# A decoder block on one core: value product and softmax sums of all attentions in one matmul group, causal maxima over 384 adjacent columns

## The chip, the cores and the metric

The kernel runs on one core of one Trainium2 chip. The metric is the device time of one execution in microseconds. Engines are called TensorE (PE in the rows; PEld is its weight load), VectorE (DVE), ScalarE (ACT), GpSimd (POOL) and SyncE (SP); SPq and ACTq in the rows are DMA issues.

## What is computed

Two decoder layers over 16 sequences of 256 tokens of 256 features, each stage followed by a residual addition and a layer norm without weights. Three of the stages are attentions:

```python
# L0 self: differential attention, 32 query heads, 8 key and 8 value heads, head size 16, causal
aw = softmax(where(tril, q @ k.T / 4, -inf))
aw = aw.reshape(B, 16, 2, S, S); aw = aw[:, :, 0] - lam * aw[:, :, 1]
y = ((aw @ v * (1 - LAMBDA_INIT)) @ Wproj) @ Wproj
# L0 cross: 16 heads of 16 against a context, no mask
out = (softmax(Q @ K.T / 4) @ V) @ w_o.T + b_o
# L1 cross: the same with biases, causal
```

The other stages (a mixture of experts behind the first cross attention, a state space layer, a feed forward with low rank experts at the end) are not touched.

## The kernel before

The stages stand one behind the other, in this order of their names: self, cross, moee, ssm, causal, ffn. `cross_attention` builds both cross and causal. In each attention a batch is one sequence. Every engine has its own program: the function `batches` calls `body(st)` once a batch, a batch in the middle in a loop of two batches an iteration, and `body` runs over the pairs i of the batch, 16 in self and 8 in cross and causal, and places the steps at fixed i. So the order on an engine is written by hand, and engines meet at semaphores alone. The stages of the work are shifted against each other: `st.has(1)` steps work on the next batch (maxima), `st.has(3)` steps on the one three ahead (projections), `st.has(-1)` and `st.has(-2)` steps on earlier ones (output product, layer norm). In self the pairs of one batch's scores begin in the middle of the body (`now`, LAG = 8).

For each pair TensorE makes the scores twice. `max_scores` writes them with queries on the partitions into one of two buffers `max_ps`; in the causal attentions the two query halves have 128 and 256 keys, and the second half begins at column 256, so a gap of 128 columns is between them. A bf16 product adds the mask on the diagonals. VectorE reduces them to `neg_max` (`take_max`; two reductions in the causal ones, of 128 and 256 columns for each of two heads). After four pairs `transpose_max` turns the maxima, ScalarE keeps them (`keep_max`), and a small DMA on ScalarE's queue (`load_row`) adds them as a row to `q_stack`. `scores` then makes the transposed scores with that row, in the single buffer `score_ps`; ScalarE writes the exponential into `probs` (`exponential`), and GpSimd clears what lies above the diagonal in the causal ones (`mask_probs`).

`weighted` multiplies a group of two pairs with matmuls of 32 output rows, one for each quarter of the partitions. A group writes its values with `v_pad` (parts 0 and 1) into the left half of `out_ps`, and the sums of its probabilities with `ones` (parts 2 and 3) into the right half. `v_pad` has for each of the two parities of a head 16 columns of values and 16 of zeros, so that two groups, one after the other, add up to 32 rows. Two groups are one tile. `keep_weighted` on ScalarE copies `out_ps` to `comb`, which frees `out_ps` for the next tile; `normalize` on VectorE takes the reciprocal of the sums and multiplies; `part_o` on GpSimd splits the result in a high and a low part for the output product (`output`, `output_1`).

On SP's queue `body` writes in cross and causal the finished rows of an earlier batch, then saves the split k, loads stacks, saves the split q and, after both saves have landed, loads the next half of the stacks (L361, L364).

## Time and profile before

| | us |
|---|---|
| median of 3 runs | 2770.53 |
| lowest and highest run | 2765.45, 2774.43 |
| span of the profiled execution | 2765.9 |
| window in the steady part of self, 100 to 660 | 560 |
| window in the steady part of cross, 820 to 1050 | 230 |
| window in the steady part of causal, 2240 to 2450 | 210 |
| TensorE busy, whole span | 2451.4 |
| VectorE busy | 1928.7 |
| ScalarE busy | 1439.0 |
| GpSimd busy | 1560.7 |

The self stage takes the time up to about 724 us, cross 724 to about 1110, causal from about 2165 to 2515. Busy times of TensorE overlap between matmuls; what a matmul group takes is best read as the distance of two starts.

### The profile page before, as it was taken

The numbers are of one execution on the slowest core, as the hardware profiler recorded it, in microseconds if no ns is written. First come the engines' busy times: TensorE is split into PE (matmuls) and PEld (weight loads), VectorE is DVE, ScalarE is ACT, GpSimd is POOL, SyncE is SP. The second block draws the span as 40 slices with busy tenths as digits, with TensorE's granted clock in tenths as the row PEclk, the third lists the DMA queues.
The fourth block names the chain that finished last, engine by engine and source line by source line (L and its number), as shares of the span: only waits on it lengthen the run. The fifth ranks groups of instructions, "written<-read, shape, count | busy, mean of one in ns | idle before, by whom it ended". The sixth has DMA issues, their size and how long they took to land. (4 is left out here: it accounts for less than half of the span.)

```text
span 2765.9 us, 66315 instructions
## 1 busy us (share of the span) xinstructions
PE 2451.4 (89%) x24760; PEld 2025.2 (73%) x24760; DVE 1928.7 (70%) x3095; ACT 1439.0 (52%) x2255; POOL 1560.7 (56%) x1873
## 2 busy tenths in 40 slices
PE   5999999999589998898999994888896799997998
PEld 4676666676466665898999993677775577765998
DVE  2567666677367786364888885999985377775776
ACT  2565565565356665433665663656563355553333
POOL 3666565666345543056666664777765477764443
PEclk9999999999799999899999997999997899998999
DMA  8565555562477873024666663111000877761111
GB/s 200 124 152 138 130 146 117 144 146 68 122 193 203 208 193 93 31 89 160 217 230 221 216 217 118 37 39 47 24 13 29 238 192 207 209 146 35 58 57 50
DMA packets 228039, 363.48 MB, mean 131 GB/s; under 512 B 52848, under 2 KB 157168, under 8 KB 220272
## 3 DMA queue, kind: packets, MB, share of 16 engines
q1 hardware_dynamic: 207248, 281.28, 38.9%
q0 software_dynamic: 17376, 78.13, 8.0%
q8 instruction: 153, 2.51, 0.4%
q10 hardware_dynamic: 3200, 1.05, 0.2%
q14 instruction: 62, 0.51, 0.1%
HBM read 231.68 MB, written 133.69 MB: 132 GB/s over the span
## 5 line engine op out<-in xcount | busy, mean ns | idle before, releaser
L1278 ACT ACTIVATE self_probs<-self_score_ps 128x768 f32<-128x768 f32 x256 | 207.7, 811 | 218.7 <-PE self_score_ps L1180 215.7
L1494 POOL TENSOR_SCALAR_AFFINE_SELECT self_probs<-self_probs 128x512 f32<-128x512 f32 x256 | 167.7, 656 | 217.6 <-ACT self_probs L1278 217.4
L1415 DVE TENSOR_REDUCE self_neg_max<-self_max_ps 128x2 f32<-128x256 f32 x256 | 108.2, 422 | 227.1 <-PE self_max_ps L1166 223.6
L722 DVE TENSOR_REDUCE cross_neg_max<-cross_max_ps 128x4 f32<-128x1024 f32 x128 | 155.9, 1222 | 70.6 <-PE cross_max_ps L500 69.6
L632 ACT ACTIVATE cross_probs<-cross_score_ps 128x1024 f32<-128x1024 f32 x128 | 131.1, 1024 | 92.9 <-PE cross_score_ps L522 92.8
L1416 DVE TENSOR_REDUCE self_neg_max<-self_max_ps 128x2 f32<-128x512 f32 x256 | 174.5, 682 | 0.0
L2206 POOL TENSOR_TENSOR moee_h_lo<-moee_h,moee_h_hi 128x512 fp32r<-128x512 f32 x78 | 112.0, 1436 | 93.0 <-ACT moee_h_hi L1943 92.3
L3501 POOL TENSOR_TENSOR ffn_g_lo<-ffn_g_full,ffn_g_hi 128x512 fp32r<-128x512 f32 x64 | 82.2, 1284 | 129.4 <-ACT ffn_g_hi L3387 117.0
L1943 ACT ACTIVATE moee_h_hi<-moee_h 128x512 fp32r<-128x512 f32 x110 | 69.5, 632 | 164.2 <-DVE moee_h L2109 158.7
L632 ACT ACTIVATE causal_probs<-causal_score_ps 128x768 f32<-128x768 f32 x128 | 103.9, 811 | 95.0 <-PE causal_score_ps L522 94.9
L1180 PE MATMUL self_score_ps<-self_q_stack,self_k_stack 49*128 49x128 f32 (+1 forms) x1024 | 131.3, 336 | 24.7 <-issue 10.3
L79 PE MATMUL moee_g_ps<-moee_x_hi,moee_in_hi 128*128 128x256 f32 x440 | 132.2, 300 | 11.1 <-DVE moee_x_lo L2096 6.9
L1180 PEld LDWEIGHTS self_score_ps<-self_q_stack,self_k_stack 49*128 49x128 f32 x1024 | 79.0, 191 | 73.6 <-issue 40.0
L2109 DVE TENSOR_TENSOR moee_h<-moee_u_ps,moee_silu 128x512 f32<-128x512 f32 x110 | 75.6, 687 | 81.2 <-PE moee_u_ps L81 77.0
L1160 PE MATMUL self_max_ps<-self_k_stack,self_q_stack 48*128 48x128 f32 (+1 forms) x1024 | 108.2, 291 | 23.0 <-POOL self_k_stack L1525 22.0
L815 POOL TENSOR_SCALAR_AFFINE_SELECT causal_probs<-causal_probs 128x512 f32<-128x512 f32 x128 | 85.0, 664 | 75.7 <-ACT causal_probs L632 71.8
L79 PE MATMUL moee_y_ps<-moee_out_hi,moee_h_hi 128*128 128x256 f32 x440 | 125.3, 285 | 1.5 <-DVE moee_out_lo L2061 1.5
L81 PE MATMUL moee_g_ps<-moee_x_hi,moee_in_lo 128*128 128x256 f32 x440 | 126.4, 287 | 0.0
L80 PE MATMUL moee_g_ps<-moee_x_lo,moee_in_hi 128*128 128x256 f32 x440 | 126.3, 287 | 0.0
L2149 POOL DMA_INDIRECT x_tiles<-kept_x,moek_slot x64 | 65.8, 1029 | 106.7 <-issue 103.0
L79 PE MATMUL moee_u_ps<-moee_x_hi,moee_in_hi 128*128 128x256 f32 x440 | 125.5, 285 | 0.0
L81 PE MATMUL moee_u_ps<-moee_x_hi,moee_in_lo 128*128 128x256 f32 x440 | 125.0, 284 | 0.0
(500 smaller groups left out, 9667.4 us busy)
## 6 DMA issues: line engine op xcount, KB each, us to landing
self_q<-self_q_split SPq DMA_DIRECT2D x48, 512.0 KB, 3.2
self_q_raw<-self_q SPq DMA_DIRECT2D x32, 768.0 KB, 7.9
cross_stacks<-cross_qk SPq DMA_DIRECT2D x64, 384.0 KB, 6.6
causal_stacks<-causal_qk SPq DMA_DIRECT2D x64, 384.0 KB, 6.6
moe_y_tiles<-lasting_y_out SPq DMA_DIRECT2D x55, 256.0 KB, 2.5
mid<-lasting_y_out SPq DMA_DIRECT2D x48, 256.0 KB, 2.2
x_tiles<-zeros SPq DMA_DIRECT2D x16, 624.0 KB, 4.5
moee_xT<-x_tiles SPq DMA_DIRECT2D x39, 256.0 KB, 7.1
```

What stands on the lines that cost most here:

```text
L79: pe.matmul(out, a[0], b[0], start=start, stop=False, **kw)
L80: pe.matmul(out, a[0], b[1], start=False, stop=False, **kw)
L81: return pe.matmul(out, a[1], b[0], start=False, stop=stop, **kw)
L632: nc.scalar.activation(probs[i // 2][:, a, :, lo:], score_ps[:, :, lo:], ACT.Exp, scale=HD ** -0.5).then_inc(prob_ready, 1)
L722: last = dve.tensor_reduce(neg_max[p][:, tile, :, col % 4, :], bank[:].rearrange("p a (q k) -> p a q k", q=QT), AX.X, ALU.max, negate=True)
L1160: last = pe.matmul(max_ps[i % 2][:, ab, q * S:q * S + (q + 1) * P], q_stack[rows, 4 * tile + c, q * P:(q + 1) * P], k_stack[p][rows, tile, ...
L1180: last = pe.matmul(score_ps[:, ab, j * S + k * P:(j + 1) * S], k_stack[p][rows, tile, k * P:(k + 1) * P], q_stack[rows, 4 * tile + c, k * P:],
L1278: nc.scalar.activation(probs[g % 4][:, a, :, P:], score_ps[:, :, P:], ACT.Exp, scale=HD ** -0.5).then_inc(prob_ready, 1)
L1415: dve.tensor_reduce(neg_max[:, tile, :, c, 0:1], bank[:, :, 0:P], AX.X, ALU.max, negate=True)
L1416: dve.tensor_reduce(neg_max[:, tile, :, c, 1:2], bank[:, :, S:2 * S], AX.X, ALU.max, negate=True).then_inc(max_kept, 1)
L1494: pool.affine_select(diagonal, diagonal, [[0, 2], [0, 2], [1, P]], ALU.is_ge, zero, base=0, channel_multiplier=-1).then_inc(prob_masked, 1)
L2206: pool.tensor_tensor(h_lo[p][f][:].rearrange("p j s -> p (j s)"), h[f][:], h_hi[p][f][:].bitcast(F32).rearrange("p j s -> p (j s)"), ALU.s ...
```

## The change

The 16 columns of `v_pad` that were zero get ones in every second column, beginning with the number of the tile. A group's product with `v_pad` now gives 16 rows of values and 16 rows that hold the sum in every second row. The groups of the two parities no longer add up; the first writes the left half of `out_ps`, the second the right half. The four matmul parts of `weighted` become two. To bring the halves together, ScalarE copies `out_ps` with its halves exchanged and scaled by a 0/1 column (`cross_weighted`, now placed ahead of `exponential` at its pair), and VectorE adds to it the other rows out of `out_ps` (`merge`, a scalar_tensor_tensor); this frees `out_ps`. GpSimd adds the sums of two tiles (`add_sums`), VectorE takes one reciprocal for both (`invert`) and `normalize` spreads a tile's half over the rows with a stream_shuffle and multiplies. `part_o` of two tiles stands at adjacent pairs.

In the causal attentions the 256 keys of the second query half now begin at column 128, and one reduction takes three blocks of 128 columns for two heads into `block_max`; after four pairs `join_max` takes the smaller negated maximum of the two blocks of the second half, and `transpose_max` waits for it.

The core of the diff (the self stage has the same edits of its functions; of it only the bodies of VectorE and GpSimd are shown, last):

```diff
@@ -531,23 +539,16 @@
                 if g == 0:
                     pe.wait_ge(v_padded, 2 * st.done(d))
                 if par == 0 and (tile or st.has(d - 1)):
-                    pe.wait_ge(comb_ready, st.at(d) * 2 + tile)
-                for part in range(4):
-                    k = part % 2
-
+                    pe.wait_ge(merged_ready, st.at(d) * 2 + tile)
+                for k in range(QT):
                     first_q = P if causal and k == 1 else 0
                     cols = slice((1 - k) * S + first_q, (2 - k) * S)
                     for quad in range(4):
                         rows = slice(32 * quad, 32 * quad + 32)
-                        if part < 2:
-                            lhs = v_pad[p][:, k, tile * 4 + quad, par, :, :].rearrange("p a e -> p (a e)")
-                            out0 = 0
-                        else:
-                            lhs, out0 = ones[:, par, :], S
-                        last = pe.matmul(out_ps[rows, out0 + first_q:out0 + S], lhs,
+                        lhs = v_pad[p][:, k, tile * 4 + quad, par, :, :].rearrange("p a e -> p (a e)")
+                        last = pe.matmul(out_ps[rows, par * S + first_q:(par + 1) * S], lhs,
                                          probs[g][:, quad % 2, quad // 2, cols],
-                                         start=(par == 0 and part == 0),
-                                         stop=(par == 1 and part == 3), skip_group_check=True)
+                                         start=k == 0, stop=k == QT - 1, skip_group_check=True)
                 last.then_inc(pv_done, 1)
@@ -632,12 +633,12 @@
                 nc.scalar.activation(probs[i // 2][:, a, :, lo:], score_ps[:, :, lo:],
                                      ACT.Exp, scale=HD ** -0.5).then_inc(prob_ready, 1)
 
-            def keep_weighted(st, d, tile):
+            def cross_weighted(st, d, tile):
                 act.wait_ge(pv_done, st.at(d) * 4 + 2 * tile + 2)
                 if st.has(d - 1):
                     act.wait_ge(o_ready, st.at(d) * 2 + tile - 1)
-                nc.scalar.activation(comb[tile][:].rearrange("p a s -> p (a s)"), out_ps[:],
-                                     ACT.Identity).then_inc(comb_ready, 1)
+                nc.scalar.activation(crossed[tile][:, ::-1, :], out_ps[:].rearrange("p (a s) -> p a s", s=S),
+                                     ACT.Identity, scale=halves[:, 1:2]).then_inc(crossed_ready, 1)
 
             def finish_rows(st):
                 n, p = st.done(-2), st.parity(-2)
@@ -651,6 +652,10 @@
 
             def body(st):
                 for i in range(PAIRS):
+                    if i == 2 and st.has(-1):
+                        cross_weighted(st, -1, 1)
+                    if i == 6 and st.has(0):
+                        cross_weighted(st, 0, 0)
                     if st.has(0):
                         exponential(st, i)
                     if i == 0 and st.has(0):
@@ -707,32 +708,61 @@
             for t in range(2):
                 dve.memset(v_pad[t][:], 0.0).then_inc(v_zeroed, 1)
             dve.wait_ge(v_zeroed, 2)
+            for t in range(2):
+                for tile in range(2):
+                    for par in range(2):
+                        ones = v_pad[t][:, :, 4 * tile:4 * tile + 4, par, 1 - par, tile::2]
+                        last = dve.memset(ones, 1.0)
+                last.then_inc(v_zeroed, 1)
 
             def take_max(st, i):
                 n, p, (tile, par, a, col) = st.at(1) * PAIRS + i, st.parity(1), place(i)
                 dve.wait_ge(max_done, n + 1)
-                if i % 4 == 0 and st.has(-1):
-                    dve.wait_ge(maxT_done, st.at(-1) * 2 + tile + 1)
                 bank = max_ps[i % 2]
                 if causal:
-                    dve.tensor_reduce(neg_max[p][:, tile, :, col % 4, 0:1], bank[:, :, 0:P], AX.X, ALU.max, negate=True)
-                    last = dve.tensor_reduce(neg_max[p][:, tile, :, col % 4, 1:2], bank[:, :, S:2 * S], AX.X, ALU.max,
-                                             negate=True)
+                    if i % 4 == 0 and (i or st.has(0)):
+                        dve.wait_ge(max_joined, st.at(1) * 2 + tile)
+                    last = dve.tensor_reduce(block_max[:, :, col % 4, :],
+                                             bank[:, :, 0:3 * P].rearrange("p a (j t) -> p a j t", t=P),
+                                             AX.X, ALU.max, negate=True)
                 else:
+                    if i % 4 == 0 and st.has(-1):
+                        dve.wait_ge(maxT_done, st.at(-1) * 2 + tile + 1)
                     last = dve.tensor_reduce(neg_max[p][:, tile, :, col % 4, :],
                                              bank[:].rearrange("p a (q k) -> p a q k", q=QT),
                                              AX.X, ALU.max, negate=True)
                 last.then_inc(max_kept, 1)
 
+            def join_max(st, tile):
+                dve.wait_ge(max_kept, st.at(1) * PAIRS + 4 * tile + 4)
+                if st.has(-1):
+                    dve.wait_ge(maxT_done, st.at(-1) * 2 + tile + 1)
+                dve.tensor_tensor(neg_max[st.parity(1)][:, tile], block_max[:, :, :, 0:2], block_max[:, :, :, 0::2],
+                                  ALU.min).then_inc(max_joined, 1)
+
+            def merge(st, d, tile):
+
+                dve.wait_ge(crossed_ready, st.at(d) * 2 + tile + 1)
+                if st.has(d - 1):
+                    dve.wait_ge(sums_ready, st.at(d))
+                    dve.wait_ge(o_ready, st.at(d) * 2 + tile - 1)
+                dve.scalar_tensor_tensor(merged[tile][:], out_ps[:].rearrange("p (a s) -> p a s", s=S),
+                                         halves[:, 0:1], crossed[tile][:], ALU.mult, ALU.add).then_inc(merged_ready, 1)
+
+            def invert(st, d):
+                dve.wait_ge(sums_ready, st.done(d))
+                dve.reciprocal(inv_sum, sums).then_inc(inv_ready, 1)
+
             def normalize(st, d, tile):
 
                 n = st.at(d) * 2 + tile
-                dve.wait_ge(comb_ready, n + 1)
-                dve.reciprocal(inv_sum[:, tile, :], comb[tile][:, 1, :]).then_inc(inv_ready, 1)
-                dve.wait_ge(inv_ready, n + 1)
+                dve.wait_ge(inv_ready, st.done(d))
+                dve.memset(gate[:], 0.0)
+                dve.stream_shuffle(crossed[tile][:, 1, :], inv_sum, [HD + tile] * HD + [tile] * HD).then_inc(scale_ready, 1)
+                dve.wait_ge(scale_ready, n + 1)
                 if st.has(d - 1):
                     dve.wait_ge(olo_ready, n - 1)
-                dve.tensor_tensor(o_full[:, tile, :], comb[tile][:, 0, :], inv_sum[:, tile, :],
+                dve.tensor_tensor(o_full[:, tile, :], merged[tile][:, 0, :], crossed[tile][:, 1, :],
                                   ALU.mult).then_inc(o_ready, 1)
 
             def norm_rows(st):
@@ -763,8 +793,18 @@
                 for i in range(PAIRS):
                     if st.has(1):
                         take_max(st, i)
+                    if causal and i % 4 == 3 and st.has(1):
+                        join_max(st, i // 4)
+                    if i == 2 and st.has(-1):
+                        merge(st, -1, 1)
+                    if i == 6 and st.has(0):
+                        merge(st, 0, 0)
                     if i == 3 and st.has(-2):
                         norm_rows(st)
+                    if i == 4 and st.has(-1):
+                        invert(st, -1)
+                    if i in (5, 6) and st.has(-1):
+                        normalize(st, -1, i - 5)
                     if i == 5 and st.has(3):
                         dve.wait_ge(xhi_ready, st.done(3))
                         dve.tensor_tensor(x_lo[:].rearrange("p k s -> p (k s)"), misc[:],
@@ -772,10 +812,6 @@
                                           ALU.subtract).then_inc(xlo_ready, 1)
                     if i == 5 and st.has(-2):
                         shift_rows(st)
-                    if i == 4 and st.has(-1):
-                        normalize(st, -1, 1)
-                    if i == 7 and st.has(0):
-                        normalize(st, 0, 0)
 
             run(dve, body)
 
                                 ).then_inc(zeroed, 1)
...
+            def add_sums(st, d):
+                pool.wait_ge(merged_ready, st.done(d) * 2)
+                if st.has(d - 1):
+                    pool.wait_ge(inv_ready, st.done(d - 1))
+                pool.tensor_tensor(sums, merged[0][:, 1, :], merged[1][:, 1, :], ALU.add).then_inc(sums_ready, 1)
...
+                    if i == 2 and st.has(-1):
+                        add_sums(st, -1)
                     if i == 0 and st.has(3) and st.has(2):
                         split_context(st)
                     if i == 2 and st.has(1):
                         pad_v(st)
-                    if i == 3 and st.has(-1):
-                        part_o(st, -1, 0)
-                    if i == 5 and st.has(-1):
-                        part_o(st, -1, 1)
+                    if i in (6, 7) and st.has(-1):
+                        part_o(st, -1, i - 6)
                     if i == 4 and st.has(-2):
                         pool.wait_ge(eps_ready, st.done(-2))
@@ -1455,21 +1522,30 @@
                 for i in range(PAIRS):
                     if st.has(1):
                         take_max(st, i)
+                    if i % 4 == 3 and st.has(1):
+                        join_max(st, i // 4)
                     if i == 1 and st.has(3) and st.has(2):
                         lower_x(st)
                     if i == 3 and st.has(-1):
                         norm_rows(st)
                     if i == 5 and st.has(-1):
                         shift_rows(st)
-                    if i in (3, 7, 11) and st.has(0):
-                        normalize(st, 0, i // 4 + 1)
+                    if i in (2, 6, 10) and st.has(0):
+                        merge(st, 0, i // 4 + 1)
+                    if i in (4, 11) and st.has(0):
+                        invert(st, 0, i // 8)
+                    if i in (5, 6) and st.has(0):
+                        normalize(st, 0, i - 5)
+                    if i == 11 and st.has(0):
+                        normalize(st, 0, 2)
+                        normalize(st, 0, 3)
+                    if i == 14 and st.has(1):
+                        merge(st, 1, 0)
...
-                    if i == 15 and st.has(1):
-                        normalize(st, 1, 0)
@@ -1546,8 +1628,10 @@
                     d, pair = now(st, i)
                     if st.has(d):
                         mask_probs(st, d, pair)
-                    if i in (0, 4, 8, 12) and st.has(0):
-                        part_o(st, 0, i // 4)
+                    if i in (2, 10) and st.has(0):
+                        add_sums(st, 0, i // 8)
+                    if i in (6, 7, 12, 13) and st.has(0):
+                        part_o(st, 0, (6, 7, 12, 13).index(i))
                     if i in (6, 8) and st.has(3):
                         split_q(st, i // 2 - 3)
```

VectorE in self, a batch's normalization at pair 11 between the maxima of pairs 11 and 12, before (`self_neg_max<-self_max_ps` are the maxima, the line is that of the kernel before):

```order
L1415 TENSOR_REDUCE self_neg_max<-self_max_ps 128x2
L1416 TENSOR_REDUCE self_neg_max<-self_max_ps 128x2
L1423 RECIPROCAL self_inv_sum<-self_comb 128x256
L1427 TENSOR_TENSOR self_o_full<-self_comb,self_inv_sum 128x256
L1415 TENSOR_REDUCE self_neg_max<-self_max_ps 128x2
```

and after, from the merge of pair 10 to the maxima behind pair 11 (lines of the kernel after):

```order
L1478 SCALAR_TENSOR_TENSOR self_merged<-self_out_ps,lasting_halves,self_crossed 128x512
L1460 TENSOR_REDUCE self_block_max<-self_max_ps 128x2x3
L1468 TENSOR_TENSOR self_neg_max<-self_block_max 128x16
L1483 RECIPROCAL self_merged<-self_merged 128x256
L1489 MEMSET self_gate 128x1
L1490 STREAM_SHUFFLE self_crossed<-self_merged 128x256
L1494 TENSOR_TENSOR self_o_full<-self_merged,self_crossed 128x256
L1489 MEMSET self_gate 128x1
L1490 STREAM_SHUFFLE self_crossed<-self_merged 128x256
L1494 TENSOR_TENSOR self_o_full<-self_merged,self_crossed 128x256
L1460 TENSOR_REDUCE self_block_max<-self_max_ps 128x2x3 x3
```

One reciprocal and one multiply of a tile stood there; now a join, a reciprocal for two tiles, and shuffle and multiply for each of them stand between two maxima, and a merge stands ahead of the maxima of pair 11.

ScalarE in cross, from the transposed maxima of pair 0 to pair 3, before:

```order
L672 ACTIVATE cross_v_full<-cross_misc 128x512
L632 ACTIVATE cross_probs<-cross_score_ps 128x1024
L622 DMA cross_stacks<-cross_max_row 1x8x128 x2
L632 ACTIVATE cross_probs<-cross_score_ps 128x1024
L639 ACTIVATE cross_comb<-cross_out_ps 128x512
L632 ACTIVATE cross_probs<-cross_score_ps 128x1024 x2
```

and after:

```order
L677 ACTIVATE cross_v_full<-cross_misc 128x512
L633 ACTIVATE cross_probs<-cross_score_ps 128x1024
L623 DMA cross_stacks<-cross_max_row 1x8x128 x2
L640 ACTIVATE cross_crossed<-cross_out_ps,lasting_halves 128x2x256
L633 ACTIVATE cross_probs<-cross_score_ps 128x1024 x3
L613 ACTIVATE cross_max_row<-cross_max_ps 16x128
```

The copy of `out_ps` (L639, now L640) has moved ahead of the exponential of pair 2.

## Rows read from the trace of the kernel before

**Rows 1.** The page, part 1: busy us, share of the span, instructions.
```profile
PE 2451.4 (89%) x24760; PEld 2025.2 (73%) x24760; DVE 1928.7 (70%) x3095; ACT 1439.0 (52%) x2255; POOL 1560.7 (56%) x1873
```

**Rows 2.** Windows: length, then PE, PEld, DVE, ACT, POOL busy, PEclk, DMA share, GB/s.
```profile
100.00:660.00 560.00, 530.23 (x6861) 388.12 (x6859) 381.03 (x681) 333.13 (x502) 348.74 (x452) 0.96 0.57 135
...
820.00:1050.00 230.00, 221.00 (x2726) 159.39 (x2722) 182.75 (x232) 148.42 (x221) 114.23 (x164) 1.00 0.77 198
...
2240.00:2450.00 210.00, 206.91 (x2682) 156.24 (x2682) 153.20 (x295) 125.28 (x227) 158.95 (x235) 1.00 0.78 204
```

**Rows 3.** Timeline, self PE: start us, us, engine, line, out<-in, xcount [idle before <-releaser].
```profile
405.27 0.86 PE L1205 MATMUL self_out_ps<-self_probs,self_v_pad 128*32 128x256 f32 x16
405.94 0.83 PE L1205 MATMUL self_out_ps<-self_probs,lasting_ones 128*32 128x256 f32 x16
406.71 0.50 PE L1180 MATMUL self_score_ps<-self_q_stack,self_k_stack 49*128 49x128 f32 x4
...
408.19 0.50 PE L1180 MATMUL self_score_ps<-self_q_stack,self_k_stack 49*128 49x128 f32 x4 [0.32 <-ACT self_probs L1278]
```

**Rows 4.** Timeline, cross PE, one weighted group.
```profile
909.34 1.07 PE L547 MATMUL cross_out_ps<-cross_probs,cross_v_pad 128*32 128x256 f32 x16
910.23 1.05 PE L547 MATMUL cross_out_ps<-cross_probs,lasting_ones 128*32 128x256 f32 x16
```

**Rows 5.** Groups of DVE in self, 200:600: busy us, mean ns | idle before.
```profile
L1416 DVE TENSOR_REDUCE self_neg_max<-self_max_ps 128x2 f32<-128x512 f32 x154 | 105.0, 682 | 0.0
L1423 DVE RECIPROCAL self_inv_sum<-self_comb 128x256 f32<-128x256 f32 x38 | 66.3, 1745 | 0.0
L1415 DVE TENSOR_REDUCE self_neg_max<-self_max_ps 128x2 f32<-128x256 f32 x154 | 65.0, 422 | 126.2 <-PE self_max_ps L1166 123.1 <-PE self_max_ps L1142 2.5
...
L1437 DVE TENSOR_TENSOR self_r<-self_misc,self_x_res 128x512 f32<-128x512 f32 x10 | 6.8, 681 | 0.0
```

**Rows 6.** Timeline, self ACT around pair 5.
```profile
391.91 2.06 ACT L1269 ACTIVATE self_q_stack<-self_q_raw 128x1024 fp32r<-128x1024 f32 x1
393.86 0.63 ACT L1301 ACTIVATE self_q_split<-self_q_full 128x512 fp32r<-128x512 f32 x1
394.38 0.81 ACT L1278 ACTIVATE self_probs<-self_score_ps 128x768 f32<-128x768 f32 x1
```

**Rows 7.** Timeline, self: POOL and PE at the edge of a batch.
```profile
416.62 1.96 POOL L1525 CAST self_k_stack<-self_k_raw 128x1024 fp32r<-128x1024 f32 x1
...
418.72 0.50 PE L1160 MATMUL self_max_ps<-self_k_stack,self_q_stack 48*128 48x128 f32 x4 [1.33 <-POOL self_k_stack L1525]
```

**Rows 8.** Timeline, cross: SP and ACT queues, then PE at the next pair 4.
```profile
914.36 0.51 SPq L396 DMA_DIRECT2D kept_x<-lasting_y_out  x1
...
918.33 0.43 SPq L375 DMA_DIRECT2D cross_qk<-cross_q_split  x1
...
925.95 0.81 SPq L364 DMA_DIRECT2D cross_stacks<-cross_qk  x2
...
919.56 1.38 ACTq L622 DMA_DIRECT2D cross_stacks<-cross_max_row  x1
...
926.31 0.50 PE L522 MATMUL cross_score_ps<-cross_stacks 49*128 49x256 f32 x4 [0.55 <-DMA cross_stacks<-cross_max_row]
```

**Rows 9.** Windows of 2 and 3 us, columns as in rows 2.
```profile
418.00:420.00 2.00, 1.28 (x11) 0.98 (x11) 1.75 (x4) 0.58 (x2) 1.53 (x3) 0.99 0.00 0
420.00:422.00 2.00, 2.00 (x15) 1.27 (x18) 0.78 (x3) 1.41 (x2) 0.94 (x3) 0.50 0.00 0
...
903.00:906.00 3.00, 2.11 (x38) 1.16 (x32) 2.89 (x8) 0.70 (x1) 0.58 (x1) 1.00 0.99 353
```

**Rows 10.** Timeline, self PE in its last batches and at its end.
```profile
645.61 0.51 PE L1180 MATMUL self_score_ps<-self_q_stack,self_k_stack 49*128 49x128 f32 x4 [0.35 <-ACT self_probs L1278]
...
649.44 0.50 PE L1180 MATMUL self_score_ps<-self_q_stack,self_k_stack 49*128 49x128 f32 x4 [0.24 <-ACT self_probs L1278]
...
715.46 0.55 PE L79 MATMUL self_misc<-self_wo_hi,self_o_hi 128*128 128x256 f32 x1 [4.45 <-POOL self_o_lo L1505]
```

137 lines of the change are left out of this document (84 added, 53 removed).

## The prediction

> **What bounds the kernel now.** I read the page's busy shares first, then the stage windows, then the timeline of one batch on each engine, and last the queues. TensorE is busy 89% of the span [rows 1], and in the steady windows of self and cross attention 530 of 560 us and 221 of 230 us; the causal one is the same with 207 of 210 us [rows 2]. A reader sees an engine with next to no idle time, so work taken from it should show. But the windows also say how far the others are: VectorE is busy 183 of 230 us in cross, and the DMA engines 0.77 of it [rows 2]. So the question is how soon something else is late.
>
> **What TensorE loses.** In self attention the product with v_pad starts at 405.27, that with the ones at 405.94, the next scores at 406.71 [rows 3]. The second product goes, so a weighted group saves 0.67 us, the distance of the two starts. In cross attention all blocks are 256 columns wide and it is 910.23 - 909.34 = 0.89 us [rows 4]. There are 128 groups in self (16 batches, 8 each), 64 in cross, 64 in causal, whose shapes are those of self: 128 x 0.67 + 64 x 0.89 + 64 x 0.67 = 186 us leave the engine. The causal maxima keep the same matmuls and only move their columns together: nothing.
>
> **What the other engines get.** Maxima: the two reductions of a pair, 0.422 + 0.682 us [rows 5], become one of 768 columns. 256 more columns cost 0.26, so 0.94; as the two now overlap by some 0.17 (the starts follow each other faster than the durations say), it saves about 0.08 a pair. Every four pairs a join of 16 columns is added behind a wait on VectorE's own last reduction: by the reduction of 256 columns [rows 5] under 0.42; being tiny, I take 0.2. Merge: 512 columns out of PSUM, as L1437, 0.68 [rows 5], on VectorE, once a tile. Reciprocals halve: 1.745 once for two tiles [rows 5]. Shuffle: no row has one. It moves 256 columns, so between 0.2 and 0.7 (a reduction of 256 and an operation of 512 columns [rows 5]), taken 0.42, with as much for the multiply behind its wait. GpSimd gets an add of 256 columns for two tiles (below the 1.96 of its 1024-column cast [rows 7]; a fourth of it and a start, 0.7) and loses as much in the v copy. ScalarE does the same copy as before, but ahead of the exponential and not behind it. Summed, VectorE has about as much as before (4 merges, 4 joins and 4 shuffles against 2 reciprocals and 16 x 0.08), but in lumps.
>
> **Self attention, walked through one batch.** A pair with a group takes 2.42 us now and 1.75 after; scores cannot follow closer than 408.19 - 406.71 = 1.48, because they wait for the exponential [rows 3]. *Pairs 3 to 8* lose three groups, 2.0 us. At pair 5 ScalarE has a sort of 2.06 and a rounding of 0.63 before the exponential of pair 6 [rows 6]; that exponential is nearly late today, and now the copy of 0.6 (as the rounding of 512 columns [rows 6]) stands ahead of it, so group 5 gives back all it saves and 0.35 more. VectorE has from pair 3 to 6 a norm, an inversion, two normalizations and a merge between its maxima; the transposed maximum of pair 8 waits 0.35 for the join. I keep 0.65 of the 2.0. *Pairs 9 to 15* lose four groups, 2.7 us. At pair 11 VectorE now runs join, inversion and two normalizations without a maximum between them: 0.2 + 1.75 + 2 x 0.84 = 3.6 us against 2.2. The maxima of pair 12 queue behind it and hold both PSUM buffers, so TensorE waits 1.5 before the maxima of pair 14; the output product then waits 0.5 for the second o_lo. I keep 0.5. *The edge and pairs 0 to 2* lose one group, 0.67; the maxima there already wait 1.33 for GpSimd's sort of k, which follows the last exponential and not TensorE [rows 7], so 0.5 of it only lengthens that wait. I keep 0.2. That is 1.2 us of 5.4 (rounded down by 0.15 for the waits I cannot place), and for 13 full batches 16 us. The last three batches have no projections and the same lumps: two pairs take 649.44 - 645.61 = 3.83 [rows 10] and will take 3.16, less 2.7 of returns a batch, so 2.7 x 3 = 8. At the stage end merge, add, inversion and two normalizations stand in a chain where a reciprocal and a multiply stood, while TensorE waits 4.45 for o_lo [rows 10]: 2.4 longer. Self: 16 + 8 - 2.4 = **22 us**. Bounds: all 5.4 a batch returned (0) and all kept (86).
>
> **Cross attention.** Here the scores of pair 4 wait for a small DMA, the row of maxima. It is issued at 919.56 and lands for the scores at 926.31, and the queue of SP, which waits for the big q write issued at 918.33, goes on at 925.95 [rows 8]: in all ten batches the two end within 0.35 us. So the row comes home with the backlog, and the backlog starts when y_out is finished, at 914.36: 12 us from there to the scores whatever TensorE does. The page DMA: Bandwidth & Descriptors of the Trainium skill, section Queues, rings and completion order, says that a DMA's semaphore write lands only after every earlier write of the same DMA engine, across its queues; by that, issuing the row sooner gains nothing, and the trace agrees with its 0.35 us. Three of the four groups (7, 1 and 3) lie inside those 12 us: their 2.67 become idle time before pair 4. The rest of the loop, from pair 4 to y_out, is 20.9 - 12 = 8.9 us and loses 0.89 with group 5, but the shift there now comes behind inversion and normalization on VectorE, which gives back 0.3. So 0.6 us a batch at full clock.
>
> The granted clock is 1.00 around today's wait of 0.5 to 1.1 us in cross, but in self it goes from 0.99 to 0.50, from 2.4 to 1.2 GHz, right behind the 1.33 us wait [rows 7, 9]. The new wait is 2.7 us. I count a fall in half of the batches, at 1.4 us each (a stretch at half clock, most of it on the path to y_out): 0.7. Net 12 x (0.6 - 0.7) = -1, plus 2 tail batches x 4 groups x 0.7 = 5.6, less 2.7 at the stage end: **2 us**. **Causal** the same way: 12 x (0.4 - 0.6) + 4 - 2.7 = **-1 us**.
>
> **Sum.** 22 + 2 - 1 = 23 us of the 186. The profiled execution's span is 2765.9, the median of the runs 2770.5; against the span that gives 2743, against the median 2748. I take 2748.
>
> **Rivals.**
> *Most of it arrives*: the lumps are hidden in the two maxima buffers and the row follows its own issue instead of the backlog. Then self keeps 4 of 5.4 a batch and cross and causal 1.8 and 1.3: 52 + 13 + 12 x 3.1 = 102, so 2670 (2620 to 2715). For it: TensorE has hardly a wait today. Against: rows 6 to 8.
> *The clock decides, slower*: the idle of 2 to 3 us before pair 4 drops the clock in every batch of cross and causal, and the longer waits of self do it half a time more. From about two falls in three on, it outweighs the gain. With 1.7 a fall: cross 12 x 1.1 = 13, causal 12 x 1.3 = 16, self 11 lost of 22: +18, 2788; with 3.4 a fall 2810. The page TensorE: Matmul & The Clock Gate of the Trainium skill, section HAM oscillation, describes such a fall in every iteration of a loop that waits for a DMA; the cross row at 903 us, at clock 1.00 with 2.11 of 3 us busy [rows 9], does not show one yet.
> *It cancels*: shuffle and merge at their upper prices lengthen the lump at pair 11 by another 0.6 and the gain of self is gone: 2770.
> *It does not do what it says*: ruled out by the order of TensorE, where the ones product is gone.
>
> **How the numbers follow.** Forecast 42% (2735 to 2764), most arrives 14%, cancels 20%, clock 24%. The range takes the forecast, the cancel case, most of the clock case and the near part of the good one: 2690 to 2800. A measurement here tells 0.3%, some 8 us, from nothing. Faster: 0.38 of the forecast, 0.14 = 0.52; same 0.25; slower 0.23.
>
> **What would show it.** Right: L547 and L1205 busy time halved, but TensorE's busy share well down from 89%; in cross an idle of 2.5 us or more before pair 4, ended by the row's DMA; in self a wait for the reduction before pair 14 and a longer one for the k sort. The clock's share tells the slower rival. Wrong: TensorE still above 93% busy in the stage windows, or the row landing sooner behind y_out than 12 us.

## The result, and the profile after

The kernel after takes 2841.8 us (median), the kernel before 2770.6 on the same chip. The ratio is 1.0255, with a 95% interval of 1.0228 to 1.0281: slower by 2.5%, where 2748 us and a small gain were forecast. Two runs at a lower granted clock, one of filler below (3711.6 us, 0.55) and one of the kernel before beside it (2851.9 us, 0.815), are in no ratio, and the first is not in the median given for filler.

| | before | after |
|---|---|---|
| median, us | 2770.6 | 2841.8 |
| span of the profiled execution | 2765.9 | 2850.8 |
| mean granted clock, share of full speed | 0.943 | 0.888 |
| up to the first `out_ps` product of self | 77.0 | 75.6 |
| self, first to last `out_ps` product | 633.7 | 693.1 |
| from there to the first one of cross | 68.3 | 73.3 |
| cross, first to last | 316.8 | 323.1 |
| from there to the first one of causal | 1093.2 | 1102.1 |
| causal, first to last | 311.6 | 315.3 |
| from there to the end | 265.3 | 268.3 |

The span is 85 us longer, and 59 of them are in self. The first line of the page and the stage windows of the kernel after, which answer to [rows 1] and [rows 2] (the last two windows are moved along with their stages; columns as there):

```profile
PE 2404.5 (84%) x20664; PEld 1982.3 (70%) x20664; DVE 1968.1 (69%) x3279; ACT 1457.1 (51%) x2255; POOL 1591.0 (56%) x1937
```

```profile
100.00:660.00 560.00, 483.14 (x4761) 352.04 (x4763) 375.01 (x659) 318.79 (x472) 330.92 (x446) 0.88 0.51 129
890.00:1120.00 230.00, 196.48 (x1965) 146.33 (x1967) 182.32 (x301) 147.30 (x215) 119.16 (x172) 0.92 0.75 196
2320.00:2530.00 210.00, 185.23 (x2034) 138.75 (x2035) 159.45 (x303) 127.69 (x224) 164.96 (x245) 0.99 0.76 203
```

4096 matmuls are gone and TensorE's busy share falls from 89% to 84%, but its busy time only by 47 us and not by 186: what is left runs slower. The granted clock of self goes from 0.96 to 0.88, that of cross from 1.00 to 0.92.

**One batch of self.** The waits of TensorE, summed over 100:660 of the kernel after (us in total, times, longest):

```profile
PE self_max_ps L1206 <- POOL self_k_stack L1607: 23.2, 12, 2.0
PE self_score_ps L1226 <- ACT self_probs L1317: 19.1, 25, 1.3
PE self_max_ps L1206 <- DVE self_block_max L1460: 17.9, 12, 1.6
PE self_misc L79 <- POOL self_o_lo L1588: 8.6, 12, 0.7
PE self_max_ps L1188 <- DVE self_neg_max L1468: 7.0, 12, 0.6
```

Before there were 14.3 us for the k sort in the same window, 10.3 with no releaser, and 5 for the exponential. Now there are five waits in each batch of 44 us: 2.0 for GpSimd's sort of k, 1.3 for the exponential of pair 6, 1.5 for the maxima buffer, 0.7 for the low part of the output product, 0.6 for the join. Windows of TensorE's clock around the k sort's wait and around the next wait for the maxima buffer (columns as in [rows 2]):

```profile
304.00:306.00 2.00, 1.21 (x11) 0.97 (x11) 0.26 (x1) 0.16 (x1) 1.23 (x2) 1.00 0.00 0
306.00:308.00 2.00, 2.00 (x20) 1.06 (x22) 1.31 (x2) 1.40 (x3) 0.27 (x1) 0.67 0.01 3
308.00:310.00 2.00, 2.00 (x21) 1.25 (x14) 0.95 (x2) 1.04 (x2) 2.00 (x2) 0.50 1.33 239
310.00:312.00 2.00, 2.00 (x11) 1.94 (x11) 1.47 (x2) 0.45 (x1) 0.92 (x2) 0.50 1.01 139
...
316.00:326.00 10.00, 8.51 (x97) 6.32 (x96) 9.60 (x23) 8.13 (x13) 4.28 (x7) 1.00 0.55 122
338.00:340.00 2.00, 0.82 (x6) 0.41 (x6) 1.95 (x3) 2.00 (x2) 1.92 (x4) 1.00 0.84 238
340.00:342.00 2.00, 1.57 (x9) 1.60 (x10) 1.35 (x2) 0.37 (x1) 0.87 (x2) 0.71 1.00 247
342.00:344.00 2.00, 2.00 (x11) 2.00 (x11) 0.00 (x0) 0.00 (x0) 0.00 (x0) 0.50 0.56 59
```

The clock falls from 1.00 to 0.50 (2.4 to 1.2 GHz) right behind each of the two waits, and stays there for some 7 and 3.5 us, in which TensorE is busy all the time. Between 100 and 660 us a fall stands behind ten of the twelve waits for the k sort (1.9 us) and behind all twelve for the maxima buffer (1.5 us), but behind one only of the twelve for the exponential (1.1 to 1.3 us). In the kernel before it stood behind seven of the eleven waits for the k sort (1.3 us). In what follows "half-clock time" is added up from windows of 1 us, where a window at 0.50 counts in full and one at 0.75 half. Between 100 and 590 us it is 41 us before and 115 after.

**The wait that the prediction missed** is at pair 6, in the batches without projections. First a steady batch, VectorE, ScalarE and TensorE of the kernel after around 322:

```profile
321.03 0.45 DVE L1490 STREAM_SHUFFLE self_crossed<-self_merged 128x256 f32<-128x256 f32 x1
...
321.61 0.43 DVE L1494 TENSOR_TENSOR self_o_full<-self_merged,self_crossed 128x256 f32<-128x256 f32 x1
```

```profile
322.07 0.69 ACT L1325 ACTIVATE self_crossed<-self_out_ps,lasting_halves 128x512 f32<-128x512 f32 x1 [0.15 <-DVE self_o_full L1494]
322.65 0.80 ACT L1317 ACTIVATE self_probs<-self_score_ps 128x768 f32<-128x768 f32 x1
```

```profile
323.51 0.51 PE L1226 MATMUL self_score_ps<-self_q_stack,self_k_stack 49*128 49x128 f32 x4 [1.28 <-ACT self_probs L1317]
```

`crossed` is the target of the copy and of the shuffle. So the copy of tile 2 (`cross_weighted`, L1325) waits for the first normalization of tile 0 on VectorE, and since it now stands ahead of the exponential, the exponential and the next scores wait too. In this steady batch the copy stands only 0.15 us for VectorE; ahead of it ScalarE is busy with the sort and the rounding of [rows 6], as the prediction walked through:

```profile
319.36 2.03 ACT L1308 ACTIVATE self_q_stack<-self_q_raw 128x1024 fp32r<-128x1024 f32 x1
...
321.29 0.63 ACT L1340 ACTIVATE self_q_split<-self_q_full 128x512 fp32r<-128x512 f32 x1
```

In two of the last batches, which have no projections to fill the time, the copy stands 2.07 us and TensorE waits 3.9:

```profile
679.81 0.69 ACT L1325 ACTIVATE self_crossed<-self_out_ps,lasting_halves 128x512 f32<-128x512 f32 x1 [2.07 <-DVE self_o_full L1494]
...
681.25 0.79 PE L1226 MATMUL self_score_ps<-self_q_stack,self_k_stack 49*128 49x128 f32 x4 [3.91 <-ACT self_probs L1317]
```

The last batches of cross and causal have it too (in causal the copy stands 4.0 us). In cross, with the clock window behind it:

```profile
1142.88 0.69 ACT L640 ACTIVATE cross_crossed<-cross_out_ps,lasting_halves 128x512 f32<-128x512 f32 x1 [3.77 <-DVE cross_o_full L765]
...
1144.54 0.80 PE L530 MATMUL cross_score_ps<-cross_stacks 49*128 49x256 f32 x4 [4.59 <-ACT cross_probs L633]
```

```profile
1143.00:1157.00 14.00, 11.66 (x81) 7.24 (x85) 5.64 (x11) 7.83 (x11) 2.96 (x5) 0.51 0.12 40
```

From the first scores of the fourteenth batch to the last scores, cross takes 57.0 us and causal 55.6, against 50.9 and 48.1 before. All fourteen kernels of this study with the new product in these stages take 52.8 to 58.3 us there in cross and 50.9 to 57.5 in causal; the four without it take 50.0 to 50.9 and 47.6 to 48.6.

**Cross.** SyncE's queue and then TensorE, one batch of the kernel after:

```profile
912.46 0.53 SPq L400 DMA_DIRECT2D kept_x<-lasting_y_out  x1
...
916.64 0.43 SPq L379 DMA_DIRECT2D cross_qk<-cross_q_split  x1
...
924.72 0.81 SPq L368 DMA_DIRECT2D cross_stacks<-cross_qk  x2
```

```profile
924.84 0.80 PE L530 MATMUL cross_score_ps<-cross_stacks 49*128 49x256 f32 x4 [2.69 <-DMA cross_stacks<-cross_max_row]
```

It is [rows 8] again: 12.4 us from y_out to the scores of pair 4, and the row's landing within 0.12 us of SyncE's. The wait is 1.6 to 2.7 us now, and half-clock stretches of 3 to 7 us stand behind nine of ten such waits between 880 and 1080 us: 34 us of half clock in 840:1050, none before.

### The profile page after: what moved, and what is told of

Same layout as the page of the kernel before. It is cut to its first block and busy times, and to the rows that moved or that the text cites. A ratio compares the mean times of both kernels' runs of the same rounds, so it can differ in the third digit from the quotient of the medians.

```text
span 2850.8 us, 58769 instructions
## 1 busy us (share of the span) xinstructions
PE 2404.5 (84%) x20664; PEld 1982.3 (70%) x20664; DVE 1968.1 (69%) x3279; ACT 1457.1 (51%) x2255; POOL 1591.0 (56%) x1937
## 5 line engine op out<-in xcount | busy, mean ns | idle before, releaser
L1460 DVE TENSOR_REDUCE self_block_max<-self_max_ps 128x6 f32<-128x768 f32 x256 | 242.5, 952 | 264.8 <-PE self_max_ps L1212 262.0
L725 DVE TENSOR_REDUCE causal_block_max<-causal_max_ps 128x6 f32<-128x768 f32 x128 | 121.8, 952 | 82.2 <-PE causal_max_ps L514 81.9
L1226 PE MATMUL self_score_ps<-self_q_stack,self_k_stack 49*128 49x128 f32 (+1 forms) x1024 | 144.5, 365 | 35.5 <-ACT self_probs L1317 31.2
L1206 PE MATMUL self_max_ps<-self_k_stack,self_q_stack 48*128 48x128 f32 (+1 forms) x1024 | 120.5, 318 | 59.3 <-POOL self_k_stack L1607 41.3
L1226 PEld LDWEIGHTS self_score_ps<-self_q_stack,self_k_stack 49*128 49x128 f32 x1024 | 88.2, 213 | 91.8 <-ACT self_probs L1317 44.2
L79 PE MATMUL moee_g_ps<-moee_x_hi,moee_in_hi 128*128 128x256 f32 x440 | 132.3, 301 | 10.3 <-DVE moee_x_lo L2180 5.5
L1206 PEld LDWEIGHTS self_max_ps<-self_k_stack,self_q_stack 48*128 48x128 f32 x1024 | 94.0, 221 | 67.2 <-POOL self_k_stack L1607 27.2
L1245 PE MATMUL self_out_ps<-self_probs,self_v_pad 128*32 128x256 f32 (+1 forms) x2048 | 129.3, 378 | 0.9 <-POOL self_probs L1570 0.5
L80 PE MATMUL moee_u_ps<-moee_x_lo,moee_in_hi 128*128 128x256 f32 x440 | 125.9, 286 | 0.8 <-issue 0.7
```

The costliest lines, as they stand in the source:

```text
L79: pe.matmul(out, a[0], b[0], start=start, stop=False, **kw)
L80: pe.matmul(out, a[0], b[1], start=False, stop=False, **kw)
L725: last = dve.tensor_reduce(block_max[:, :, col % 4, :], bank[:, :, 0:3 * P].rearrange("p a (j t) -> p a j t", t=P), AX.X, ALU.max, negate= ...
L1206: last = pe.matmul(max_ps[i % 2][:, ab, q * P:q * P + (q + 1) * P], q_stack[rows, 4 * tile + c, q * P:(q + 1) * P], k_stack[p][rows, tile, ...
L1226: last = pe.matmul(score_ps[:, ab, j * S + k * P:(j + 1) * S], k_stack[p][rows, tile, k * P:(k + 1) * P], q_stack[rows, 4 * tile + c, k * P:],
L1245: last = pe.matmul(out_ps[rows, par * S + first_q:(par + 1) * S], lhs, probs[g % 4][:, quad % 2, quad // 2, cols], start=k == 0, stop=k == ...
```

## The experiments

Two theories were set against each other. **Clock:** the work taken away turned into waits, behind which the rest runs at half clock. **Chain:** the new steps (copy ahead of the exponential, merge, join, inversion, shuffles) set the period, whatever TensorE does. Beside each run the kernel before was timed on the same chip, and its time stands next to the ratio; all are medians. Where an edit is shown for self alone, what it does in cross and causal stands in the expectation.

### The work put back, and the two halves apart

product_twice:

```diff
-                for k in range(QT):
+                for k in 2 * tuple(range(QT)):
```

> The kernel after, in which each group's product with v_pad is made twice in all three attentions (the second pass starts anew and overwrites the first), so TensorE has as many matmuls as the kernel before, and all other new steps stay. Theory clock: the removed work turned into waits of 1.3 to 2.7 us, behind each of which TensorE runs at half clock for 4 to 8 us; with the work back the waits shrink, the clock stays up, and the time is about that of before, 2765 to 2800, self ending near 715. Theory chain: the new steps on VectorE and ScalarE set the period whatever TensorE does; the time stays at 2840 or rises by a part of the 186 us, 2840 to 2950.

Measured: 2819.4 against 2768.9, ratio 1.017 (1.015 to 1.020). Granted clock 0.934; half-clock time in 100:590 is 21 us, against 115. With 186 us more work (estimated in the prediction) than the kernel after it is 22 us faster. Self is 661 us: 32 of the 59 lost come back as the half-clock time goes, 28 stay lost with all the work in place. The time lies between the two ranges, so both theories hold a part. Cross (325) and causal (327) are no shorter. The clock windows of self, 100:660:

```profile
100.00:660.00 560.00, 514.33 (x6625) 372.43 (x6623) 393.54 (x691) 329.37 (x487) 345.69 (x464) 0.98 0.55 134
```

maxima_only: `block_max`, one reduction and the join put into the kernel before, products as before.

> The kernel before with the maxima half of the change alone (384 gapless columns, one reduction a pair, a join every four pairs); values and sums are made by two products as before. Theory clock: TensorE loses nothing, so no new waits; 2760 to 2780. Theory chain: the join puts VectorE 0.2 to 0.4 us later at each transposed maximum, 64 + 32 of them: up to 2800.

Measured: 2768.6, ratio 1.000 (0.999 to 1.002). The maxima half is worth nothing by itself.

product_only: the kernel after with the two reductions and without join.

> The kernel after without the maxima half (two reductions a pair, no join). If the product half alone makes the loss (both theories say so, most of it): 2825 to 2855. If the join behind the last reduction has a large part in it: 2780 to 2815.

Measured: 2850.2, ratio 1.028 (1.026 to 1.031). The product half makes the whole loss.

### The waits, one by one

copy_behind:

```diff
-                    if i in (2, 6, 10) and st.has(0):
-                        cross_weighted(st, 0, i // 4 + 1)
...
                     if st.has(d):
                         exponential(st, d, pair)
+                    if i in (2, 6, 10) and st.has(0):
+                        cross_weighted(st, 0, i // 4 + 1)
```

> The kernel after with ScalarE's copy of out_ps (cross_weighted) behind the exponential of its pair, as before, not ahead of it. In the trace of after this copy waits at pair 6 of self for the first normalization on VectorE, and the exponential behind it makes TensorE wait 1.3 us a batch, 3.9 in the last three. If that wait is on the path: 13 x 1.3 + 3 x 3.9 = 28 us less, near 2813. If the time goes into the other waits (k sort, maxima of pair 14) as soon as this one is gone: 2830 to 2845.

Measured: 2809.4 against 2768.9, ratio 1.014 (1.008 to 1.020): 32 us less than the kernel after, near the 28 counted from the trace, though its runs spread over 32 us (2793 to 2825). Self is 670 us, 23 less. The two waits at the batch's edge are as they were (25 and 19 us in 100:660), half-clock time 107.

filler:

```diff
-                for k in range(QT):
+                for k in (1 + 2 * (g in (1, 2))) * tuple(range(QT)):
```

> The kernel after with repeated products only just ahead of the waits: in self the groups of pairs 13 and 15 are made three times (ahead of the waits for the maxima buffer and for the k sort), in cross the group of pair 3 three times and in causal twice (ahead of the wait for the row's DMA). It adds 2 x 2 x 0.67 = 2.7 us of TensorE work a batch in self, 1.8 in cross, 0.7 in causal, which lies in waits of 1.5 to 2.7 us. Theory clock (a fall to half clock follows such a wait): the falls behind these waits go, the half-clock time in self drops from 225 us to under 110, self gets 30 to 60 us shorter though it has 43 us more work, and cross some 15: 2765 to 2800. Theory chain: nothing gets shorter, work that does not fit into the waits is added: 2841 to 2870.

Measured: 2795.8 against 2779.1, ratio 1.009 (1.006 to 1.013), at the upper end of the clock theory's range. Self is 648 us, 45 less than after, with 43 us more work in it; cross is 315, 8 less. The half-clock time of 100:590 is 17 us. Nothing but TensorE's own work was changed: this shows the clock. The new steps are all still there; TensorE spends its repeats where it waited for them. Its waits of 1.1 to 1.3 us for the exponential of pair 6 stay, and no fall stands behind any of the twelve between 100 and 600 us.

sortk_early: `if i == 15` becomes `if i == 14` for GpSimd's `sort_k`.

> The kernel after with GpSimd's sort of k in self one pair earlier (at 14, not at 15). In the trace of after TensorE waits 1.9 us for it at each edge of two batches and runs some 8 us at half clock behind that. If the wait goes and its fall with it: 15 x (1.9 + 3 to 4) = 75 to 90 less, 2750 to 2765. If the wait goes but the next one behind it (the maxima, the exponential) takes its place and the clock falls there: 2810 to 2840. If the sort of k only follows its data: no change, 2841.

Measured: 2791.9 against 2779.1, ratio 1.005 (1.003 to 1.008). Self falls by 52 us to 641, though causal of this profile is 10 us longer. GpSimd's order now; the next batch's maxima start at 291.85 on TensorE, without a wait:

```profile
285.78 0.64 POOL L1570 TENSOR_SCALAR_AFFINE_SELECT self_probs<-self_probs 128x512 f32<-128x512 f32 x1
286.37 2.00 POOL L1607 CAST self_k_stack<-self_k_raw 128x1024 fp32r<-128x1024 f32 x1
293.04 0.64 POOL L1570 TENSOR_SCALAR_AFFINE_SELECT self_probs<-self_probs 128x512 f32<-128x512 f32 x1 [4.67 <-ACT self_probs L1317]
```

The sort waited for nothing that pair 15 makes; it only stood behind its mask. Most batches go from 44.3 to 40.3 us. Not all of the expected 75 to 90 us came: the waits for the maxima buffer and the exponential stand, and so does the half clock behind them (100 us in 100:590).

three_moves, the moves of copy_behind and sortk_early, with the last normalization moved too:

```diff
                     if i == 11 and st.has(0):
                         normalize(st, 0, 2)
+                    if i == 12 and st.has(0):
                         normalize(st, 0, 3)
```

> The kernel after with three moves: ScalarE's copy behind the exponential, GpSimd's k sort at pair 14, and VectorE's fourth normalization of self at pair 12 and not 11. Each takes one of the named waits of TensorE in self (1.3, 1.9 and 1.5 us a batch). If these waits and the falls behind them are what self lost: self back to 600 to 630 us, total 2735 to 2775. If VectorE's total work or another chain takes over: 2790 to 2810, no better than the copy's move alone (2809).

Measured: 2758.5 against 2779.1, ratio 0.993 (0.990 to 0.996). Self is 610 us, 83 less than after. Half-clock time of 100:590 is 40 us. What is late now is the output product, 1.8 us a batch for `o_lo`.

three_moves_filler has the repeats of filler on top.

> The three moves and the repeated products ahead of the waits together. Theory clock: the moves shorten the waits and the repeats keep the clock up in what is left of them, the sum of both gains: 2730 to 2765. Theory chain: as the three moves alone or up to 40 us longer.

Measured: 2780.1 against 2779.1, ratio 1.001 (0.999 to 1.003). The two gains do not add: the repeats no longer lie in waits, and self is 633 us, with 38 us of half clock in 100:590, as in three_moves (40).

### What is worth anything without the change

store_last moves `kept_x <- y_out` and its wait to the end of SyncE's batch in cross and causal.

> The kernel after with SyncE's store of finished rows at the end of its batch in cross and causal, behind the saves of the split k and q and the loads of the stacks, not ahead of them. In the trace of after the DMA queues stand idle for some 4 us until y_out is finished, since everything behind the store in SyncE's program waits with it, and the row of maxima lands 12.4 us after that. If the 12 us leg starts at y_out (the prediction's reading): the leg starts 2 to 4 us earlier, TensorE's wait before pair 4 (1.5 to 2.7 us) and the fall of the clock behind it go, cross 323 to near 300 us and causal 315 to near 295: 2795 to 2815. If the row waits for its own maxima or the bandwidth of the burst: 2835 to 2845.

Measured: 2825.5 against 2772.9, ratio 1.019 (1.016 to 1.022). That is 10 us over the range. Cross is 301 us, 22 less than after; a batch takes 19.2 us against 21.3 (before: 20.8). Causal does not get shorter (321 here, 311 in all_moves), so its half of the expectation fell. Self is 682 us in this profile and 693 in that of the kernel after, with the same program in self: differences of some 10 us in self between two profiles tell nothing. SyncE and TensorE in cross:

```profile
879.04 0.38 SPq L379 DMA_DIRECT2D cross_qk<-cross_q_split  x1
879.46 0.55 SPq L406 DMA_DIRECT2D kept_x<-lasting_y_out  x1
...
885.83 1.23 SPq L368 DMA_DIRECT2D cross_stacks<-cross_qk  x2
```

```profile
886.56 0.50 PE L530 MATMUL cross_score_ps<-cross_stacks 49*128 49x256 f32 x4 [1.29 <-DMA cross_stacks<-cross_max_row]
```

The saves no longer wait for y_out. The row still comes home with the backlog (0.7 us apart), but that starts earlier. The row's wait in 230 us goes from 23.2 to 13.2 us.

before_both: the kernel *before*, with the k sort at pair 14 and the store last.

> A control: the kernel before, with the two moves that have nothing to do with the change: GpSimd's k sort of self at pair 14 and SyncE's store of finished rows last in its batch. If the kernel before is bound by TensorE, it gains at most its own waits: 1.3 us a batch in self and their falls (some 20 to 35 us), 0.5 to 1.1 a batch in cross (5 to 10 us): 2725 to 2750. If these moves are worth nothing there: 2765 to 2775.

Measured: 2739.7 against 2772.9, ratio 0.990 (0.987 to 0.993). Self is 606 us, with all its products in it, a batch 37.9 us against 40.8. It has no wait for the k sort left:

```profile
PE self_score_ps L1180 <- issue: 10.0, 3, 3.8
PE self_score_ps L1180 <- ACT self_probs L1278: 6.4, 23, 0.3
PE self_max_ps L1160 <- DVE self_neg_max L1416: 0.7, 2, 0.3
```

all_moves adds to three_moves the store last and the output product of self at pair 15.

> The kernel after with all moves: the copy behind the exponential, the k sort at pair 14, the fourth normalization at pair 12, the first output product of self at pair 15 instead of 14 (it waited 2.2 us a batch for the low part with the three moves), and the store of finished rows last. If the removed 186 us of TensorE work count once the waits are gone: self 590 to 600, cross near 300, causal near 295: 2700 to 2730, well under the kernel before. If the chain of normalization and output product sets the period of self: self stays at 610, 2725 to 2745.

Measured: 2750.8 against 2772.9, ratio 0.992 (0.989 to 0.994), 6 us over the worse of the two ranges. Cross 298.5, self 620: the output product at 15 took its wait away and gave others of 0.5 us at two places of every batch. Whether it helps is not shown: the first twelve batches of self take 468 us here, and 462 (three_moves) and 473 (tail_twice) without it. So after five moves the change was still no better than the kernel before with two.

tail_twice tried the last batches of self, where three_moves stands like this:

```profile
600.00:608.00 8.00, 4.85 (x56) 2.83 (x53) 7.85 (x18) 5.59 (x7) 3.67 (x7) 0.99 0.94 182
608.00:628.00 20.00, 19.50 (x143) 11.99 (x144) 13.89 (x26) 9.18 (x15) 12.41 (x20) 0.50 0.09 29
...
640.00:650.00 10.00, 6.98 (x73) 3.88 (x71) 9.79 (x23) 6.71 (x9) 5.01 (x9) 0.77 0.19 69
650.00:670.00 20.00, 19.90 (x140) 13.14 (x139) 12.29 (x20) 7.36 (x11) 9.86 (x14) 0.52 0.19 59
```

and before_both like this:

```profile
600.00:630.00 30.00, 28.35 (x399) 19.43 (x399) 24.34 (x46) 18.19 (x26) 20.71 (x29) 1.00 0.45 94
630.00:670.00 40.00, 37.65 (x535) 25.76 (x537) 30.44 (x54) 22.38 (x35) 21.37 (x30) 1.00 0.14 48
```

Behind a stretch with 3 us of waits TensorE is busy for 20 us at half clock. In before_both there are twelve waits of 0.24 to 0.35 us and one of 0.7 in these 70 us, and the clock stays at 1.00. The page TensorE: Matmul & The Clock Gate of the Trainium skill, section A second HAM failure mode: psum-queue depth-cycling, describes a kernel whose clock swings because TensorE idles briefly and often between its groups; this second trace also idles briefly and often, and its clock does not swing.

> The kernel after with the three moves and the store of finished rows last (self as in three_moves, cross and causal as in store_last), and in self the product made twice only in batches without projections, the last three. In three_moves TensorE runs some 50 us of the last two batches at half clock and a batch takes 40 us, against 34 in before_both, where the ones product is still there. Theory clock: with that work back these batches take 34 to 35 us and self falls from 610 to near 598: 2720 to 2735. Theory chain (merge, add, inversion, shuffle, multiply): 40 us stay or grow: 2740 to 2755.

Measured: 2745.8 against 2772.1, ratio 0.989 (0.987 to 0.992); the last three batches take 41, 38 and 34 us, in three_moves 40, 40 and 30. No gain, though the half-clock time of the last three fell from 52 to 17 us: the clock is not what holds them alone.

tail_and_one, in place of that edit in tail_twice:

```diff
-                for k in range(QT):
+                for k in (1 + (not st.has(3) or g == 1)) * tuple(range(QT)):
```

> As tail_twice, and in all batches of self the group of pair 13 twice too, ahead of the 2.2 us wait for the low part of the output product. Theory clock: 0.67 us more in a wait that it shortens; the falls of the steady batches (75 us of half clock in 560) get fewer, 0.5 to 1 us a batch: 2710 to 2730. If the fall is set off by the small waits elsewhere: as tail_twice or up to 8 us longer.

Measured: 2731.9 against 2772.1, ratio 0.985 (0.982 to 0.987). Self is 599 us; the first twelve batches take 37.2 to 39.9 us from first scores to first scores, five of them under 37.5, and the half-clock time of 100:590 is 17 us. Its last three batches, in which TensorE has as much work as in before_both, settle what tail_twice left open. Windows from the first scores of the fourteenth batch to the last ones, here and in before_both:

```profile
562.00:669.00 107.00, 92.26 (x1253) 63.87 (x1249) 75.92 (x140) 58.46 (x85) 66.02 (x92) 1.00 0.29 75
```

```profile
580.00:679.00 99.00, 93.24 (x1301) 64.99 (x1301) 71.94 (x130) 57.28 (x84) 62.03 (x85) 1.00 0.32 81
```

The clock is at 1.00 in both, and 8 us more are needed here: TensorE waits 4.5 us for the merge and 3.9 for `o_lo`, and for neither in before_both. three_moves takes 113 us for the same stretch, with 52 us of half clock and less work.

mix: self of before_both, cross and causal of the kernel after with the store last.

> Self attention of the kernel before (two products, two reductions) with the k sort at pair 14; cross and causal of the kernel after, with the copy behind the exponential and the store last. It tells where the change itself is worth something: if in cross, 298 to 301 us against 310 of before_both and 317 of before, it comes to 2722 to 2735, under before_both (2740). If cross and causal gain only from the store's move, as before_both: 2736 to 2745.

Measured: 2737.6 against 2772.1, ratio 0.988 (0.985 to 0.991). Cross is 300.6 against 310.4 of before_both: there the change gains 10 us. The total does not show them and lies in the range of "no gain"; in this profile self, whose program is the same, is 5 us longer than in that of before_both, and the stretch between cross and causal 7.

one_only and, beside it on the same chip, before_both again:

> The kernel after with the three moves, the store of finished rows last, and in self the group of pair 13 made twice in all batches; no other repeats. In tail_and_one this single repeated group held the clock (17 us of half clock in 490 against 40 to 64) and the batch at 37.2 us; the doubled last batches were worth nothing there (41, 38 and 34 us against 40, 40 and 30). Expected: steady batches 37.2, self 595 to 603, 2722 to 2735. If the doubled last batches did hold something: 2735 to 2745.

> The control before_both once more (the kernel before, k sort at pair 14, store last), on the same chip and beside the same runs as one_only, to tell the two apart. 2735 to 2745. If one_only is under it by more than 8 us, the change is worth something once it is placed well; if not, the two moves alone are the better kernel.

Measured: one_only 2727.5, ratio 0.984 (0.982 to 0.987); before_both_again 2740.8, ratio 0.988 (0.986 to 0.990). So the change, with four moves and one repeated group, is 13 us better than the kernel before with the two moves that apply to it. Self windows of one_only:

```profile
100.00:590.00 490.00, 448.39 (x5064) 322.77 (x5064) 367.39 (x674) 316.78 (x479) 343.77 (x456) 0.99 0.61 150
590.00:670.00 80.00, 69.69 (x649) 44.62 (x649) 53.86 (x103) 40.58 (x58) 43.30 (x62) 0.74 0.13 40
```

It is the fastest kernel of this study, 1.6% under the one before.

## Why the prediction was wrong

**What held.** TensorE's share fell, and the busy time of the product was near halved (self 230 to 129 us, cross 137 to 73). Prices: block reduction 0.95 (0.94 said), merge 0.74 (0.68), shuffle 0.44 (0.42), join 0.17 where it stands alone (0.2), copy 0.69 (0.6), `add_sums` 0.73 (0.7). The lump at pair 11 came as walked through: from the join at 333.97 to the next maxima at 337.88 it is 3.9 us (3.6), the wait for the maxima buffer 1.5 (1.5), that for `o_lo` 0.7 (0.5). The 12 us leg of cross was 12.4, with a wait of 1.6 to 2.7 us (2.7). In a steady batch the pair 6 came as walked through too: a wait of 1.28 us where a return of 0.67 and 0.35 was counted.

**What failed: the clock in self.** The forecast priced falls in cross and causal and none in self, although [rows 7] and [rows 9] showed one in self, behind a wait of 1.3 us. A steady batch of self now takes 44.3 us against 40.8. Its parts: 5.4 us of work less; waits of 6.6 us against some 1.7, so 4.9 returned, where 4.2 were forecast; half-clock time of 10.4 us a batch against 3.4, and half of the difference is lost, 3.5. The sum is +3.0 of the measured 3.5. Waits alone would have left a gain of half a microsecond. filler shows that this term is the clock: it adds 2.7 us of work a batch and the batch gets 4.5 shorter. In all, the first thirteen batches of self lose 37 of the 59 us, where 16 of gain were forecast.

**What failed next: the batches without projections.** The forecast gave them the removed product as a gain, 8 us in self, 5.6 in cross and 4 in causal. These last three batches lost 22, 6.1 and 7.5 instead. It priced the copy at pair 6 by its length of 0.6 us in self, not at all in the last batches of cross and causal, and nowhere by its wait: ahead of the exponential it waits for VectorE's normalization, 2.1 us in self, 3.8 in cross and 4.0 in causal where no projection fills the time, and half clock follows. copy_behind takes that order back and gets 32 us, 23 of them in self: 17 in the twelve batches from the second on, where TensorE waits 1.1 to 1.3 us at this pair, and 6 in the last three.

In self the last three batch lengths are 45.9, 46.6 and 30.4 against 35.8, 37.3 and 27.6. With the moves made, tail_and_one shows 8 us left at full clock, which are the waits for the merge and `o_lo`; three_moves loses some 6 more with half clock. In cross and causal this was not taken apart.

**The stage end** of self: the wait for `o_lo` is 7.8 us against 4.45 [rows 10], 3.4 longer (2.4 said).

**Cross.** The wait was right and the clock's share too small: a fall in nine batches of ten and not in half. The 34 us of half clock would be 1.7 us a batch if all of it were on the path. filler, with none in cross, takes 20.0 us a batch (from the second to the fourteenth), against 21.0 after and 20.7 before: 0.7 of gain without the clock (0.6 said) and 0.9 lost with it (0.7 said). "Whatever TensorE does" was right for the row, but y_out was taken as its natural start. store_last shows that only SyncE's order made it so. With that the change gains in cross, 300 against 310 us.

**Causal** came out 4 us slower (1 said), against a spread of 306 to 326 us between profiles. Its batches up to the fourteenth are as long as before (20.4 against 20.5 us); the last three are 7.5 us longer.

**Between the stages.** Of the 5 us ahead of cross, 3.4 are the wait for `o_lo` above; the memsets of ones in `v_pad` lie there too, which was not tried apart. At the ends of cross and causal the same wait is 7.4 us against 5.7, 1.7 longer (2.7 said); it stands in the 9 us between cross and causal and in the 3 behind causal. The rest of the 9 is open: the stretch varies from 1091 to 1106 us.

**The rival** "The clock decides, slower" named the mechanism, with 24%. It stood at 2788 to 2810, since it let self fall only "half a time more". The measured time is 32 us past its end. Its sum was also added up too low: with 3.4 us a fall its own terms give 12 x 2.8 + 12 x 3.0 - 11 = 59, which is 2829 and not 2810.

The page DMA: Bandwidth & Descriptors of the Trainium skill, section Queues, rings and completion order, was cited for the row that lands with the backlog. The traces of after and of store_last agree, with 0.12 and 0.7 us between the two.

## What to carry to other kernels

When work is taken off an engine that is 89% busy, list every wait that grows and read from the trace what the clock does behind such a wait *today*, and count the fall in every stage that shows one. The length alone does not tell: here a fall stood behind 22 of 24 waits of 1.5 to 2.0 us, seven of eleven of 1.3 us at one place, and one of twelve of 1.1 to 1.3 us at another. Before taking work away, take the waits away: moving one sort and one store gave 33 us to the kernel before, more than 186 us of removed matmuls gave in any version without repeated work. And a step moved ahead of a critical one brings its own waits along, not only its length; look for them in the last batches, where other work no longer hides them.
